# First attention: one masked minimum over a wide row's scores in two neighbouring PSUM banks, in place of a partial and a masked one

## The reference, cut to what matters

```
Q = (xn @ Wq.T).reshape(b, 16, 1024, 16)      # 2 x 16 = 32 heads, 16 wide
K, V in the same way
scores = einsum('bhqd,bhkd->bhqk', Q, K)       # causal: keys after the query are masked
weights = softmax(scores / sqrt(16))
ctx = einsum('bhqk,bhkd->bhqd', weights, V)
```

## Time and profile before

| | us |
|---|---|
| median of 3 executions | 1458.79 |
| lowest and highest | 1451.10, 1460.52 |
| the profiled execution's own time | 1457.44 |
| its span, first to last instruction | 1455.6 |
| mean granted TensorE clock | 0.913 |

### The profile page before, as it was taken

One profiled execution on the slowest core, in us unless ns is written; L12 is line 12 of the kernel. 1 busy time (PEld: TensorE's weight loads), 2 busy tenths in 40 slices (PEclk: granted clock), 3 DMA queues, 4 the chain that ended last, 5 costly groups with the idle time before them and its releaser, 6 DMA issues. The chain is left out here.

```text
span 1455.6 us, 22062 instructions
## 1 busy us (share of the span) xinstructions
PE 1216.7 (84%) x7424; PEld 865.7 (59%) x7424; DVE 879.4 (60%) x2322; ACT 739.0 (51%) x1683; POOL 519.8 (36%) x546
## 2 busy tenths in 40 slices
PE   2684937898999987685859999999999999999979
PEld 2574834343434375574747776777777676776667
DVE  7664627888888613343456667666666666766501
ACT  1451701677777605434346566656656666666400
POOL 0130413433342100312305555555555455555200
PEclk9796965889999798797989999999999999999989
DMA  2222348567771074101030101111111111110082
GB/s 86 91 88 62 144 60 71 53 64 88 85 86 16 1 204 155 34 29 38 27 93 20 33 29 41 41 41 41 41 41 41 41 27 29 52 30 15 16 291 70
DMA packets 118011, 91.48 MB, mean 63 GB/s; under 512 B 47696, under 2 KB 107536, under 8 KB 117648
## 3 DMA queue, kind: packets, MB, share of 16 engines
q1 hardware_dynamic: 116864, 89.09, 27.7%
q10 hardware_dynamic: 1040, 1.05, 0.2%
HBM read 51.05 MB, written 30.67 MB: 56 GB/s over the span
## 5 line engine op out<-in xcount | busy, mean ns | idle before, releaser
L763 POOL TENSOR_SCALAR a_p<-a_p,a_rl 128x128 f32<-128x128 f32 (+7 forms) x256 | 216.7, 848 | 340.9 <-DVE a_rl L705 340.8
L746 ACT ACTIVATE a_p<-psum,a_nm 128x128 f32<-128x128 f32 (+7 forms) x256 | 189.7, 741 | 111.8 <-DVE a_nm L699 111.3
L1246 ACT ACTIVATE a_pt<-psum 128x512 f32<-128x512 f32 (+3 forms) x384 | 168.3, 492 | 88.2 <-PE psum L1109 84.8
L796 PE MATMUL psum<-ident,a_p 128*128 128x128 f32 x1152 | 171.5, 276 | 22.5 <-DVE a_pt L732 22.5
L1099 PE MATMUL psum<-a_op_k,a_op_q 64*128 64x512 f32 (+3 forms) x384 | 137.0, 456 | 31.1 <-POOL a_op_k L1041 30.0
L818 PE MATMUL psum<-a_pt,v 128*64 128x256 f32 (+1 forms) x1280 | 160.1, 372 | 0.6 <-ACT a_ot L832 0.6
L796 PEld LDWEIGHTS psum<-ident,a_p 128*128 128x128 f32 x1152 | 129.6, 141 | 46.2 <-issue 39.1
L699 DVE CUSTOM_DVE_ANT_0 psum<-psum,mask_a 128x128 f32<-128x128 f32 (+3 forms) x128 | 63.5, 496 | 139.2 <-PE psum L781 139.1
L1109 PE MATMUL psum<-a_op_q,a_op_k 64*128 64x512 f32 (+3 forms) x384 | 131.6, 429 | 9.8 <-ACT a_pt L1246 7.4
L730 ACT ACTIVATE a_pt<-psum 128x256 f32<-128x256 f32 (+2 forms) x192 | 87.3, 455 | 87.9 <-PE psum L796 86.8
L1109 PEld LDWEIGHTS psum<-a_op_q,a_op_k 64*128 64x128 f32 x384 | 65.1, 201 | 106.2 <-ACT a_pt L1246 84.0
(11 more groups left out here) (291 smaller groups left out, 2775.2 us busy)
## 6 DMA issues: line engine op xcount, KB each, us to landing
a_swap<-w_p SPq DMA_DIRECT2D x64, 128.0 KB, 2.3
ot_d<-a_ot SPq DMA_DIRECT2D x16, 512.0 KB, 2.6
o_ot<-ot_d SPq DMA_DIRECT2D x8, 1024.0 KB, 8.5
a_raw_q<-qk_d SPq DMA_DIRECT2D x48, 128.0 KB, 5.2
a_raw_k<-qk_d SPq DMA_DIRECT2D x48, 128.0 KB, 9.4
w<-wf_d SPq DMA_DIRECT2D x16, 384.0 KB, 3.4
qk_d<-p_stage_h SPq DMA_DIRECT2D x8, 512.0 KB, 2.7
qk_d<-p_stage_l SPq DMA_DIRECT2D x8, 512.0 KB, 3.4
```

The costliest lines, as they stand in the source:

```text
L746: e.activation(s.p[:, t % NPB, 0:(i + 1) * P], C.score[t % 2][:, 0:(i + 1) * P], ACT.Exp, scale=-1.0, bias=s.nm[:, k:k + 1], accum_out=s.l ...
L763: e.tensor_scalar(s.p[:, t % NPB, 0:(i + 1) * P], s.p[:, t % NPB, 0:(i + 1) * P], s.rl[:, k:k + 1], 1.0, ALU.mult, ALU.mult).then_inc(s.no ...
L796: ins = e.transpose(C.turn[par][:, (k - k0) * P:(k - k0 + 1) * P], s.p[:, tt % NPB, k * P:(k + 1) * P], C.ident[:, :])
L1246: e.activation(pt[:, k // G0 % NPT, hd, off:HALF], bank_b("score", g, k)[:, off:HALF], ACT.Exp, scale=-1.0).then_inc(exped, 1)
```

## The change

- `UNITS_A` is reordered so that the two halves of a wide row are neighbours (slots 2n and 2n+1); the narrow ones come in runs of two of one head. `UNITS_B` takes the four heads in plain order, so that the two units of a slot still use different halves of the operand rows.
- A new `place_a` gives banks: a wide row takes banks 0 and 1 or banks 2 and 3, skipping a bank where the ring's position is odd. `HELD_A` holds, for each user, the last user of its bank, where the last user of both banks of a wide row is its second unit.
- `minimum` does nothing for w = 0. For w = 1 it waits for both scores and takes one masked minimum over 640 to 1024 columns across the two banks, starting from a constant, with a new 1024-column `mask` in SBUF (a memset and a copy on VectorE at the stage's start). `part` goes. `a_maxed` now counts 32 minima for a group in place of 48.

```
-UNITS_A = [(2 * blk + a, i, 0) for a in range(2) for i in range(4) for blk in (1, 0)]
-UNITS_A += [(2 * blk + a, i, w) for a in range(2) for i in range(4, NT) for w in range(2) for blk in (1, 0)]
-UNITS_B = [(c, j, 2 * blk + a) for c in range(NCH) for j in range(4 * c + 4) for a in range(2) for blk in (0, 1)]
+UNITS_A = [(2 * blk + a, i + n, 0) for a in range(2) for i in (0, 2) for blk in (1, 0) for n in range(2)]
+UNITS_A += [(2 * blk + a, i, w) for a in range(2) for i in range(4, NT) for blk in (1, 0) for w in range(2)]
+UNITS_B = [(c, j, hd) for c in range(NCH) for j in range(4 * c + 4) for hd in range(G0)]
+MINIMA = G0 * NT
+def minima_by(k):
+    return sum(i < 4 or w == 1 for _, i, w in UNITS_A[:k])
-A_END = (4 * G0, SLOTS)
+A_END = (4 * G0, MINIMA)
-AT_A = {u: r for r, u in enumerate(RING_A)}
+def place_a():
+    at, held, last, r = {}, {}, [None] * 4, 0
+    for user in RING_A:
+        if user in at:
+            continue
+        kind, g, k = user
+        together = [user]
+        if kind == "score" and UNITS_A[k][1] >= 4:
+            together.append((kind, g, k + 1))
+            r += r % 2
+        for each in together:
+            at[each], held[each] = r % 4, last[r % 4]
+            last[r % 4] = together[-1]
+            r += 1
+    return at, held
+AT_A, HELD_A = place_a()
...
                 def free_a(*user):
-                    r = AT_A[user] - len(a_banks)
-                    if r >= 0:
-                        kind, g, n = RING_A[r]
+                    if HELD_A[user]:
+                        kind, g, n = HELD_A[user]
                         if kind == "score":
-                            e.wait_ge(a_maxed, g * SLOTS + n + 1)
+                            e.wait_ge(a_maxed, g * MINIMA + minima_by(n + 1))
...
                     hd, i, w = UNITS_A[k]
+                    if i >= 4 and w == 0:
+                        return
                     e.wait_ge(a_scored, g * SLOTS + k + 1)
-                    n = min((w + 1) * HALF, (i + 1) * P) - w * HALF
-                    bank = bank_a("score", g, k)
-                    if i >= 4 and w == 0:
-                        e.tensor_reduce(part[:, hd, i - 4:i - 3], bank[:, 0:n], AX.X, ALU.min).then_inc(a_maxed, 1)
-                        return
-                    so_far = -MASKED
-                    if w:
-                        e.wait_ge(a_maxed, g * SLOTS + k - 1)
-                        so_far = part[:, hd, i - 4:i - 3]
-                    e.tensor_tensor_reduce(out=bank[:, 0:n], in0=bank[:, 0:n], in1=C.mask_a[:, HALF - n:HALF], scale=1.0,
-                                           scalar=so_far, op0=ALU.add, op1=ALU.min,
+                    n = (i + 1) * P
+                    first = AT_A["score", g, k] - w
+                    scores = C.score[first // 2][:, 0:n] if w else a_banks[first][:, 0:n]
+                    e.tensor_tensor_reduce(out=scores, in0=scores, in1=mask[:, T - n:T], scale=1.0,
+                                           scalar=-MASKED, op0=ALU.add, op1=ALU.min,
                                            accum_out=nm[:, hd, i:i + 1]).then_inc(a_maxed, 1)
...
                 e.memset(raw[1][:, :, :], -1.0).then_inc(cleared, 1)
+                e.memset(mask[:, 0:T - HALF], 0.0).then_inc(mask_made, 1)
+                e.tensor_copy(mask[:, T - HALF:T], C.mask_a[:, :]).then_inc(mask_made, 1)
+                e.wait_ge(mask_made, 2)
```

More of the change, by code:

```diff
@@ L936, in attend0 @@
         pt = ph.sb("pt", [P, NPT, G0, HALF])
-        part = ph.sb("part", [P, G0, 4])
         nm = ph.sb("nm", [P, G0, NT])
@@ L947, in attend0 @@
         v_landed = [ph.sem(f"v{u}_landed") for u in range(3)]
+        mask = ph.sb("mask", [P, T])
+        mask_made = ph.sem("mask_made")
         cleared = ph.sem("cleared")
@@ L971, in bank_a @@
         def bank_a(*user):
-            return a_banks[AT_A[user] % len(a_banks)]
+            return a_banks[AT_A[user]]
         def bank_b(*user):
@@ L1180, in minimum @@
                     hd, i, w = UNITS_A[k]
+                    if i >= 4 and w == 0:
+                        return
                     e.wait_ge(a_scored, g * SLOTS + k + 1)
-                    n = min((w + 1) * HALF, (i + 1) * P) - w * HALF
-                    bank = bank_a("score", g, k)
-                    if i >= 4 and w == 0:
-                        e.tensor_reduce(part[:, hd, i - 4:i - 3], bank[:, 0:n], AX.X, ALU.min).then_inc(a_maxed, 1)
-                        return
-                    so_far = -MASKED
-                    if w:
-                        e.wait_ge(a_maxed, g * SLOTS + k - 1)
-                        so_far = part[:, hd, i - 4:i - 3]
-                    e.tensor_tensor_reduce(out=bank[:, 0:n], in0=bank[:, 0:n], in1=C.mask_a[:, HALF - n:HALF], scale=1.0,
-                                           scalar=so_far, op0=ALU.add, op1=ALU.min,
+                    n = (i + 1) * P
[3 more added lines that the diff above has]
+                                           scalar=-MASKED, op0=ALU.add, op1=ALU.min,
                                            accum_out=nm[:, hd, i:i + 1]).then_inc(a_maxed, 1)
                 def cut(g, c):
-                    e.wait_ge(a_maxed, g * SLOTS + A_END[c])
+                    e.wait_ge(a_maxed, g * MINIMA + A_END[c])
                     wait(e, m_turned, 2 * g + c)
```

## The result

The changed kernel takes 1482.28 us (median of 4 executions, 1478.81 to 1485.52) beside 1457.38 for the kernel before: a ratio of 1.0176, 95% interval 1.0133 to 1.0218. It is slower, clear of the noise, by 24.9 us, where 14.4 were forecast. The profiled execution's own time is 1483.16 us, its span 1481.4, its mean granted clock 0.907.

The account below looks back on a forecast made before the run. TensorE's fixed order was taken as the bound with both passes, VectorE in iteration -1, GpSimd's mask in 2 to 4. Iterations' 1.1 + 2.15 + 3.65 + 1.1 + 2.8 + 3.65 = 14.4 us gave 1473, range 1460 to 1483.

Parts of the forecast that it names:

- VectorE's saving: Wide rows' minima: one merged operation saves 0.08 us a row, 10 us over 128 rows, worth next to nothing.
- The pairing's cost: Iterations with both passes: TensorE waits where an output transpose leaves one pair of banks, 3.65 us an iteration.
- Slots 18 to 22: At `turn_back`: transposes wait for row (16, 17), slot 20 for row (18, 19); slot 22 starts 1.5 us later.
- slot 28: At `turn_output`: one bank of the free pair is taken, so the slot waits for row (26, 27), +0.8 us.
- slots 35 to 37: At `turn_back`: slot 36 waits for row (34, 35), so slot 37 goes 1.15 us later.
- slots 0 to 10: Slots 0 to 3 wait for the last two wide rows instead of single banks: 0.3 us later.
- to first issue: Iteration -1, pass A alone, at half clock: TensorE cannot refill a pair within one row, +1.1 us, bounds -1.3 and +3.
- Iterations 2 to 4: The delay first fills the 2.1 us TensorE stands at slot 41 for GpSimd's mask: +0.4 us each, together 1.1.
- Iteration 7: Last iteration, pass B alone: no pass A in it, so nothing was added to the sum.
- rival D: TensorE's clock falls oftener: three more half-clock stretches, 3 us each, beside the forecast, 1482 us; chance 0.08.
- B: VectorE is the bound after all and passes its saving on: -6 to -10 us, 1449 to 1453; chance 0.07.
- C: TensorE's waits are half hidden, by loads pacing iterations 1 to 5 and shorter VectorE lag: +3 to +10 us; chance 0.15.

Follow-up runs that it names:

- after_again: The changed kernel run once more with nothing altered: 1482.39 us, ratio 1.0193 to the kernel before.
- before_drained: The kernel before with three waits added on TensorE, at slots 20, 28 and 36, until VectorE has finished every unit issued so far: ratio 1.0030.
- before_moved: The kernel before with all output transposes moved to slots where pass A has narrow rows: 1462.98 us, ratio 1.0037.
- before_waits: The kernel before, with each masked minimum of a wide row also waiting for the minimum just ahead of it on VectorE: ratio 1.0110.

## Why the prediction had the pairing right and failed on the clock

The direction was right, and so was the mechanism of the pairing. The forecast was 1473, and the range to 1483 holds 1482.3 by less than 1 us. The likeliest outcome given, within 1% of no change (0.54), was not what came, and 24.9 us came where 14.4 were summed. The step that failed is the clock's, which the sum has at nothing.

**VectorE's saving** (0.08 us a row, worth next to nothing): too small, and right in its worth. From start to start a row of 640 columns takes 0.74 us, 896 take 1.02 and 1024 take 1.15, each some 0.05 under the estimate, so a row saves 0.13 us from start to start, 16 us in all in place of 10. VectorE's busy time fell by 8.4 us only, since rows that stand apart no longer overlap and the new mask is in it. TensorE gained nothing by it.

**The pairing's cost** (3.65 us in a full iteration): right, event by event. Slots 18 to 22 +1.4 (1.5 said, of which a step of 0.04 from 459.70 + 0.59 to 460.33 has no row), slot 28 +0.8 (0.8), slots 35 to 37: 0.56 us before, 421.81 to 423.34 after, +1.0 (1.15), slots 0 to 10 +0.4 (0.3). An iteration at full clock takes 33.2 us; 33.0 was said. That it is the transposes' doing was shown twice: left out (28.0 beside 28.2), and moved (30.3 beside 30.6, and 1466 in place of 1482).

**By iteration**, with 0.35 us taken off for each microsecond at 0.50:

| | to first issue | 0 | 1 | 2 to 4 | 5 | 6 | 7 | sum |
|---|---|---|---|---|---|---|---|---|
| forecast | 1.1 | 2.15 | 3.65 | 1.1 | 2.8 | 3.65 | 0 | 14.4 |
| profile after | 1.5 | 0.2 | 2.9 | 4.4 | 2.8 | 3.2 | 1.3 | 16.3 |
| `after_again` | 1.3 | 2.4 | 3.5 | 4.0 | 3.0 | 3.1 | 1.3 | 18.6 |

Iterations 2 to 4 stand 3 us above the forecast here, and it isn't shown that the step "iteration 6's period with the full delay, 33.0, against 32.6: +0.4 each" is the one at fault. The wait for the mask did go, as forecast (0.2 us for it in iteration 4 of the profile after). The one pair at full clock on both sides is iteration 2 of the kernel before and of `after_again`: 32.6 and 33.2, +0.6. The 4 us come from the other two periods of the kernel before, 32.5 and 32.8 with 3.4 us of half clock each, which the 0.35 turns into 31.3 and 31.6. They are within 0.2 us of the one at full clock, so the half clock may have cost them nothing there. At +0.6 each the sums are 13.7 and 16.4 in place of 16.3 and 18.6. Iteration 0's 0.2 in the profile after has a cast in it that is 1.3 us shorter, which is not the change's doing (see the last section). Iteration 7's 1.3 is no work of the change; it is within what the 0.35 leaves uncertain, with 31 us at 0.50.

**The clock** (rival D, 0.08): this is the term that failed. "Nothing in the rows speaks for its happening oftener than now." It did happen oftener: 127.4 and 115.4 us at 0.50 in the stage in place of 93.5, which at 0.35 is 8 to 12 us, the rest of the 24.9 or most of it; the means over all executions give 7 to 10. About half of this lies in iteration 7, which "has no pass A" and stands at 0 in the sum: it took 6.0 us more in both traces, with 30.7 us at 0.50 in place of 17.1, and 13.6 us at 0.35 are 4.8. And the trace before did speak for it, had I read the clock beside the earlier trace rows: the kernel before loses its clock behind the wait at slot 41 in two of three iterations, and a change that puts 3.8 us of standing into each iteration may bring more such places. The sum had to carry a term for that; I had it as a small chance beside the sum.

**Rivals B and C** fell: TensorE waits for VectorE 5.5 us an iteration, and the full-clock iterations show the whole of the delay.

**What stays open.** What brings the clock down. Long stalls were followed by a fall in many cases, at their own place; three short ones in an iteration did not lengthen the half clock (75 us); without the transposes, with less work for TensorE, it was longer (136); with 0.11 to 0.14 us waits on VectorE it was too (110); and of two equal stretches one was followed by a fall and one was not. In iteration 7, where no stall of pass A is left, it was 0 in `before_drained`, 17.1 in the kernel before, and 30.7 both in the changed kernel and in `before_moved`, which has no pairs; no run shows what decides that. So that the pairing's stalls cause the longer half clock is argued, not shown. The shares of the loss, 14 to 19 us of standing and 7 to 12 of clock, rest on one slope and two profiles.

## What to carry to other kernels

Merging two operations over two banks into one saves the engine's fixed cost but makes the two banks one resource, released at the end; count what else uses that ring, since one user of a single bank between two pairs leaves one pair and turns a pipeline into a series. Look at what the merged engine waits for before paying for its speed: here it had no one waiting (0.2 us). And when a change makes TensorE stand longer in an iteration, give the clock a term in the sum, with bounds, from the places where the profile already shows it fall behind a stall.

## What the runs showed of the hardware

An instruction of VectorE can be held by GpSimd's memsets. At the end of iteration 0 a cast of 16 columns, some 0.17 us elsewhere (407.47 in the profile after), took 3.35 us in the kernel before and 2.02 in the changed one. The kernel before, VectorE, then GpSimd:

```profile
285.39 3.35 DVE L1200 CAST a_m_hl<-a_nm 128x16 fp32r<-128x16 f32 x1
```

```profile
284.70 1.38 POOL L1345 MEMSET w1n<- 128x1536 f32 x1
286.01 1.38 POOL L1345 MEMSET w2n<- 128x1536 f32 x1
287.33 1.38 POOL L1345 MEMSET w3n<- 128x1536 f32 x1
```

The cast ends at 288.74, the last memset at 288.71. In the changed kernel it runs from 286.27 to 288.29, and the second memset ends at 288.27. In all 17 traces the cast of that place is long, 0.74 to 3.50 us, and ends 0.02 to 0.03 us behind the end of one of the three memsets. Behind which one isn't the change's doing: in `after_again` it took 3.33 us. So 1.3 us of iteration 0 differ between two traces of one kernel, a term that no step of the prediction had. The Trainium skill, SBUF — State Buffer, Who interferes with whom, says that a cast may use the port pair that VectorE shares with GpSimd, and that the engine which has the pair then blocks the other fully. The rows agree, and show more: the cast can be held over two or three memsets in a row, and in `before_waits` (0.74 us) it got in behind one, with the third still to come.

The clock's price is low for this kernel, 0.31 to 0.39 us of time for a microsecond at half speed. The likely reason, argued and not tested, is that pass B is paced by ScalarE's exponentials as well: in iteration 7 at full clock TensorE is busy 24.5 of 29.9 us and ScalarE 20.9.
